# A graph-attention and expert kernel on one Trainium2 core: setup transfers of 125 rows cut in 112 and 13, one queue for x, stores and weights, and the first three pairs summed in plain fp32 with row releases of their own

## The reference, cut to what matters

```python
x = x + gnn(layernorm(x), dist, W, att_src, att_dst, src, dst)      # x: 6250 x 256, 106250 edges
x = x + ffn(layernorm(x)[None], Wr, br, W1, b1, g1, be1, m1, v1, W2, ..., Wo, bo)[0]

def gnn(feat, ...):                       # 4 heads of 64
    ft = (feat @ W).reshape(n, 4, 64)
    e = leaky_relu(e_src[src] + e_dst[dst], 0.2)      # e_src, e_dst: ft times an attention row, summed per head
    ex = exp(e - segment_max(e, dst)[dst])
    a = ex / segment_sum(ex, dst)[dst] * dist
    return segment_sum(ft[src] * a, dst)              # dst is sorted

def ffn(x, ...):                          # 8 experts, all of them for every row
    w = softmax(x @ Wr + br)
    h = relu(bn(x @ W1[e] + b1)); h = relu(bn(h @ W2[e] + b2)); y = h @ Wo[e] + bo
    return sum over e of y[e] * w[e]
```

## Time and profile before

| | before |
|---|---|
| median of 3 runs | 1673.95 us (1670.68 to 1675.28) |
| profiled execution, its own time | 1672.18 us |
| its span, first to last instruction | 1670.6 us |
| TensorE busy | 1488.4 us, 89% of the span |
| VectorE, ScalarE, GpSimd busy | 1213.7, 777.6, 1028.3 us |
| moved by DMA | 187.48 MB, mean 112 GB/s |
| mean granted TensorE clock | 0.954 |

### The profile page before, as it was taken

The page is one execution under the profiler, slowest core; times in us unless marked ns, Lnnn a source line. Parts: engine busy times, 40 slices in busy tenths (PEclk is TensorE's granted clock), DMA queues, the critical chain, the costliest instruction groups (busy, mean ns, idle before and its releaser), DMA issues.

```text
span 1670.6 us, 23915 instructions
## 1 busy us (share of the span) xinstructions
PE 1488.4 (89%) x8358; PEld 1292.6 (77%) x8358; DVE 1213.7 (73%) x2207; ACT 777.6 (47%) x1353; POOL 1028.3 (62%) x926
## 2 busy tenths in 40 slices
PE   2664035999999999999999999999999999999998
PEld 2442034888888888888888888888888888888887
DVE  3333266887888888888888888788778877887751
ACT  1232013455545554555555545555555555455543
POOL 1000777777777777777777777777777777777000
PEclk9887556999999999999999999999999999999999
DMA  3332934444443444344444444444444344433000
GB/s 116 104 103 79 303 111 112 128 115 129 111 128 103 129 112 128 103 129 112 122 112 121 118 115 119 114 123 111 123 115 125 106 125 114 125 105 109 20 0 13
DMA packets 106040, 187.48 MB, mean 112 GB/s; under 512 B 38454, under 2 KB 70475, under 8 KB 105890
## 3 DMA queue, kind: packets, MB, share of 16 engines
q0 software_dynamic: 43664, 121.77, 26.5%
q1 hardware_dynamic: 55264, 57.76, 11.5%
q10 hardware_dynamic: 6992, 6.42, 1.3%
HBM read 172.72 MB, written 14.42 MB: 112 GB/s over the span
## 4 chain that ended last, share of the span: by engine, by line
PE 66%; DVE 11%; issue 7%; DMA 6%; POOL 4%; ACT 4%; SPq 0%; DVEq 0%; ACTq 0%; POOLq 0%
PE bankH L701 33%; PE bankY L730 16%; PE bankE L660 5%; PE bankE L661 5%; POOL gath L565 4%; DMA gath<-in_x 4%; ACT msg_hi L866 3%; DVE onehot L1237 2%; PE bankE L596 2%; PE bankB L646 1%; DVE x L1348 1%; DVE stats L1297 1%; DVE x L1295 1%; DVE x L1291 1%; PE bankA L678 1%
## 5 line engine op out<-in xcount | busy, mean ns | idle before, releaser
L565 POOL DMA_INDIRECT gath<-table,src_win x900 | 1020.9, 1134 | 502.4 <-issue 229.4
L894 ACT ACTIVATE h<-bankH,bn_shift,bn_scale 128x250 f32<-128x250 f32 x800 | 401.5, 552 | 424.6 <-PE bankH L701 424.3
L701 PE MATMUL bankH<-h,w 128*128 128x250 f32 x1600 | 446.6, 398 | 0.0
L730 PE MATMUL bankY<-wo,h 128*125 128x256 f32 x1600 | 378.1, 379 | 1.1 <-DVE x L1348 1.1
L701 PE MATMUL bankH<-xT,w 128*128 128x250 f32 x1600 | 375.2, 377 | 0.1
L1279 DVE TENSOR_TENSOR msg_lo<-gath,msg_hi 128x2340 fp32r<-128x2340 f32 x100 | 259.5, 2595 | 114.3 <-ACT msg_hi L866 114.3
L730 PEld LDWEIGHTS bankY<-wo,h 128*125 128x125 f32 x1600 | 296.0, 187 | 42.5 <-issue 1.4
L866 ACT ACTIVATE msg_hi<-gath 128x2340 fp32r<-128x2340 f32 x100 | 215.1, 2151 | 233.0 <-PE bankE L661 229.6
L701 PEld LDWEIGHTS bankH<-xT,w 128*128 128x128 f32 x1600 | 294.2, 190 | 30.4 <-ACT h L894 0.2
L701 PEld LDWEIGHTS bankH<-h,w 128*128 128x128 f32 x1600 | 278.4, 198 | 18.0 <-issue 0.2
L1348 DVE SCALAR_TENSOR_TENSOR x<-bankY,gate,x 125x256 f32<-125x256 f32 x400 | 173.9, 475 | 136.4 <-PE bankY L730 136.4
(11 more groups left out here) (164 smaller groups left out, 870.1 us busy)
## 6 DMA issues: line engine op xcount, KB each, us to landing
onehot_t<-dst_low SPq DMA_DIRECT2D x50, 576.0 KB, 5.2
gath<-table,src_win POOLq DMA_INDIRECT x900, 2.8
x_res<-in_x SPq DMA_DIRECT2D x27, 250.0 KB
table<-gath SPq DMA_DIRECT2D x25, 253.9 KB
out<-x SPq DMA_DIRECT2D x25, 250.0 KB
gath<-in_x SPq DMA_DIRECT2D x23, 250.0 KB
w<-in_L_ffn_W ACTq DMA_DIRECT2D x2, 2048.0 KB, 21.6
wo<-in_L_ffn_Wo ACTq DMA_DIRECT2D x1, 2048.0 KB, 37.3
```

The source lines that it names most:

```text
L565: pool.indirect_dma_start(gath[:, g.slot(u), t, :], None, table, bass.IndirectOffsetOnAxis(src_win[:, g.win, u, t:t + 1], 0)).then_inc(row ...
L701: mm = pe.matmul(target[:, hc * 2 * NT:(hc + 1) * 2 * NT], weights[:, e * KC + c, hc * P:(hc + 1) * P], operand(c), start=(c == 0), stop=( ...
L730: mm = pe.matmul(bankY[0:NT, u * D:(u + 1) * D], h2[:, e % 2, c, u, :], wo[:, e * KC + c, :], start=(c == 0), stop=(c == KC - 1))
L894: ins = act.activation(target[:, e % 2, hc, :, :].rearrange("p u n -> p (u n)"), source[:, hc * 2 * NT:(hc + 1) * 2 * NT], ACT.Relu, bias= ...
```

## The change

Setup:
- x is loaded in six groups of 1, 1, 2, 4, 8 and 9 pairs, issued at the start with no waits between them, each cut in 112 and 13 rows; stores are cut in the same way. Small parameters and the weights move to SP's queue, the weights in twelve parts of 0.5 MB behind the stores of pairs 4 to 15. W and the attention rows move to ScalarE's queue.
- The norm is two pairs behind the moments, `project` has two sets of banks, and TensorE and ScalarE are one pair further apart. VectorE's steps for edges and factors are spread over pairs 3 to 21 (`aside`).
- GpSimd loads the windows and dst_low of pair 0 itself, before it waits for the stores.

Main part:
- Stage n=-2 is replaced by `first`, which also makes the edge terms of pair 1.
- Pairs 0 to 2 are summed in plain fp32 straight from the gathered rows: one matmul a column and no `keep_high` and `low_part`.
- `Plan` moves steps: for pairs 1 and 2 the run maxima, carries and logits come in the stage in which the pair is g, at s=2 and 3 (pair 1) and 1 and 2 (pair 2), after `layer1` of the pair before has begun. From pair 3 on all is as before.
- The 36 rows of pairs 1, 2 and 3 are released by lists of events.

```diff
+NATIVE = 3
+ROWS_CUT = ((0, 112), (112, NT))
+X_GROUPS = (0, 1, 2, 4, 8, 16, 25)
+SOON = ((2, (0,)), (3, (1,)), (4, (2,)), (5, (3,)))
+STEADY = Plan(0, dict(SOON), 1, 3, {3: (0,), 4: (1,), 5: (2,), 6: (3,)}, {5: (0,), 6: (1,)}, 7)
+PLANS = {0: Plan(0, dict(SOON), 1, 3, {3: (0,), 4: (1,), 5: (2,), 6: (3,)}, {5: (0,), 6: (1,)}, 6, low=False),
+         1: Plan(3, {5: (0,), 6: (1, 2, 3)}, 4, 5, {6: (0,), 7: (1, 2, 3)}, {7: (0, 1)}, 8, runs=2, low=False),
+         2: Plan(2, {4: (0, 1), 5: (2, 3)}, 3, 4, {5: (0, 1), 6: (2, 3)}, {5: (0,), 6: (1,)}, 7, runs=1, low=False)}
...
+        def load_x(eng, k):
+            lo, hi = X_GROUPS[k:k + 2]
+            for p0, p1 in ROWS_CUT:
...
+                eng.dma_start(target, x.rearrange("(k p) d -> p k d", p=NT)[p0:p1, lo * 2:hi * 2, :]).then_inc(t_x[k], 16)
...
             def store_rows(g):
                 sp.wait_ge(t_kept, g.n * 2 + 2)
-                sp.dma_start(table_pairs[g.n], ft_rows[0:NT, g.par, :, :]).then_inc(t_stored[g.par], 16)
+                for p0, p1 in ROWS_CUT:
+                    sp.dma_start(table_pairs[g.n, p0:p1], ft_rows[p0:p1, g.par, :, :]).then_inc(t_stored[g.par], 16)
+            def store_and_load(g):
+                store_rows(g)
+                i, q = divmod(g.n - WEIGHTS_AT, 4)
+                if 0 <= i < 3:
+                    buf, dram = ((w1, W1), (w2, W2), (wo, Wo))[i]
+                    sp.dma_start(buf[:, q * 4:q * 4 + 4, :], ...).then_inc(weights_in, 16)
...
             general(pool, path)
-            pool.wait_ge(setup_done, 1)
+            load_window(pool, Pair(0))
+            pool.wait_ge(low_stored, 32)
+            for u in range(2):
+                load_low(pool, Pair(0), u)
+            pool.wait_ge(t_stored[0], 32 * ((NP + 1) // 2))
+            pool.wait_ge(t_stored[1], 32 * (NP // 2))
+            second = released((
+                (carry_ready, 1, 2), (logit_ready, 1, 2), (ex_ready, 1, 3), (msg_ready, 1, 2), (msg_ready, 2, 2), (msg_ready, 3, 2),
+                (onehot_ready, 5, 2), (msg_ready, 4, 2), (var_ready, 1, 3), (onehot_ready, 7, 2), (var_ready, 2, 2), (xn_ready, 2, 1),
+                (xT_ready, 1, 3), (rexp_ready, 1, 2), (h1_kept, 2, 2), (h2_kept, 1, 2), (h1_kept, 3, 2)))
...
             def project(g):
                 pe.wait_ge(t_xT, g.n + 1)
-                if not g.begins(1):
-                    pe.wait_ge(t_rows, g.n * 2)
+                if not g.begins(2):
+                    pe.wait_ge(t_rows, (g.n - 1) * 2)
...
-                        mm = pe.matmul(bankE[u][0:NT, 0:ROWX], xT[:, g.par, c, u, :], wx[:, c, :],
+                        mm = pe.matmul(t_bank[g.par][u][0:NT, 0:ROWX], xT[:, g.par, c, u, :], wx[:, c, :],
...
             def aggregate(g, c):
+                if g.begins(NATIVE):
+                    pe.wait_ge(msg_ready, g.n * CHUNKS + c + 1)
+                    u, cols = c // 2, (c % 2) * TC
+                    for t in range(TC):
+                        mm = pe.matmul(bankE[u][0:NT, 0:ROW], onehot[:, c, t, :].bitcast(F32), gath[:, g.slot(u), cols + t, :],
+                                       start=(cols + t == 0), stop=(cols + t == TE - 1))
+                    mm.then_inc(agg_done, 1)
+                    return
...
+                    if late(g) and s == plan.logits:
+                        turn_carry(g)
...
+                    if late(g) and s == plan.runs:
+                        turn_runs(g)
```

More of the change, by code:

```diff
@@ L412, in load_dst_low @@
             def load_dst_low(a, u):
[L414 to L418, removed]
+                sp.wait_ge(edge_done, a.tile(u) - 1)
+                load_low(sp, a, u)
             def store(f):
@@ L515, in pace @@
+            assert len(second) == len(third) == len(fourth) == 2 * TE
             def pace(g, row):
-                if g.begins(1):
+                if g.n in early:
+                    event = early[g.n].get(row)
+                    if event is not None:
+                        pool.wait_ge(*event)
                     return
[L519 to L545, removed]
@@ L546, in pace @@
-                if r or not rows:
+                f, step, kind, r = Pair(g.n - 3), FROM, 0, row
+                while r >= BEHIND[step % EX][kind]:
+                    r -= BEHIND[step % EX][kind]
+                    step, kind = (step, kind + 1) if kind < 3 else (step + 1, 0)
+                f, step = f + step // EX, step % EX
+                if r:
                     return
@@ L737, in nothing, with first @@
                 pass
+            def first(a):
+                turn_bounds(None, a)
+                for _ in to_edges(a):
+                    pass
+                ahead = to_edges(a + 1)
+                for _ in range(TE):
+                    next(ahead)
+                turn_runs(a)
+                turn_carry(a)
+                for _ in ahead:
+                    pass
             def body(f, g, a):
-                small = to_edges(a) if a is not None else iter(())
+                small = to_edges(a) if f is not None and a is not None else iter(())
+                plan = plan_of(g)
                 def between():
@@ L790, in _ @@
             general(pe, path)
-            over_stages(NP, body)
+            over_stages(NP, first, body)
             last = Pair(NP - 1)
@@ L940, in path @@
+                    if late(g) and s == plan.logits:
+                        exp_logits(g)
+                    if g is not None and plan.low:
+                        for c in plan.sums.get(s + 1, ()):
+                            keep_high(g, c)
             def path():
@@ L1390, in body @@
                         edge_sum(a)
                         carries(a)
-                    if f is not None and (s >= 2 or not f.begins(1)):
+                    if run and (s >= 2 or not f.begins(1)):
                         add_y(*before(f, s, 2))
-            over_stages(NP, body)
+                    if late(g) and s == plan.runs:
+                        runs(g)
+                    if late(g) and s == plan.logits:
+                        weigh(g)
+            over_stages(NP, first, body)
```

603 lines of the change are left out of this document (354 added, 249 removed).

## The result

| | before | after |
|---|---|---|
| median | 1672.50 us (4 runs, 1670.68 to 1675.28) | 1622.04 us (4 runs, 1620.49 to 1624.87) |
| ratio to before, 95% interval | | 0.9705 [0.9692, 0.9718] |
| profiled execution, span | 1670.6 us | 1620.1 us |
| first gather of pair 0 | 165.6 us | 115.0 us |
| from there to layer 1 of pair 0 | 110.1 us | 81.5 us |

The kernel became 50.5 us faster. That is inside the range and 24 us above the number. So setup holds most of the miss.

The account below looks back on a forecast made before the run. TensorE bounds the main part, and x on one queue with a third of the DMA engines bounds setup; -70.6 - 26 + 13.5 + 7 = -76.1 us, giving 1596.1 profiled and 1598 us predicted, range 1577 to 1632.

Parts of the forecast that it names:

- The cut: Setup loads and stores: 125 rows use 5 of 16 DMA engines, 112 rows use 16 and 13 rows 13.
- First gather at 95: End of setup: pair 0's first gather at 95 us against 165.58, -70.6 us; bounds 84 and 118.
- the 7.5 put down for stalls in it: Setup loop: 3 us for an emptied buffer, 1.5 for small matmuls, 3 for stores with weight parts.
- Pair 0 to layer 1 at 84: First gather to layer 1 of pair 0: 84 us against 110.1, -26 us; bounds -30 and -12.
- The end of the bounds at which all sums run at half clock: Pair 0's sums: 36 matmuls at 0.9 us, 32 us for 18.5, leaving a gain of only 12 us.
- Plain fp32 +13.5: Sums of pairs 1 and 2 in TensorE-bound stages: 16 us a pair against 9.4, +13.5 us for both.
- New waits +7: First main stages: 3.5 us at `turn_runs(1)` and 3.5 for pair 1's chunks, norm and messages; bounds 0 and 25.
- The slower: Setup: the cut doesn't raise the queue's 103 GB/s, first gather at 190, 1693 us; chance 0.02.
- no-gain cases: Setup: the cut brings nothing and the order hides it, first gather near 165, 1670 us; chance 0.01.
- TensorE's half clock: Setup: half clock throughout bounds it, first gather 49 us later, 1647 us; chance 0.07.
- The second rival: Setup: the queue bounds it at 157 GB/s, first gather at 127, 1630 us; chance 0.10.
- The releases: Pairs 1 and 2: event-held rows starve gathers, costing 45 us instead of 7, 1636 us; chance 0.09.

Follow-up runs that it names:

- e1: The kernel before with only its setup x loads and table stores cut in 112 and 13 rows; 1626.8 us.
- e2: The kernel after without the cut, loads and stores of 125 rows again; 1669.8 us.
- e4: e3 with the 16 small parameter loads issued from ScalarE's queue behind the attention rows; 1613.4 us.
- e3: The kernel after with the last x group (9 pairs) loaded in three parts behind the first stores; 1614.2 us.
- e7: e4 without the event lists that hold back the gathers of pairs 1 to 3; 1608.8 us.
- e8: e7 with VectorE's one-hots and scans of pair 3 ahead of pair 2's residual and norm; 1602.9 us.
- e6: e5 with maxima, carries and logits of pairs 1 and 2 back in their old stage, plain fp32 kept; 1620.0 us.
- e5: The kernel after without the event lists that hold back the gathers of pairs 1 to 3; 1615.0 us.

## Why the prediction was right, and where it was off

**The cut (right).** That transfers of 125 rows kept a third of the engines busy, and that this bounded setup, is what e1 and e2 show, from both sides. That it was 5 engines is read from the share (0.33 and 0.34) and the rule cited above; no trace names them.

**First gather at 95 (off by 20, setup's gain mis-sized).** The term that failed is the start of the loop, "All of x needs 21 us and is far ahead of its use". TensorE turns pair 5 from 53.43 us; at the forecast pace, with the first product done at 19, it would have begun at 19 + 4 x 2.65 = 29.6. Of these 24 us 8 were lost before pair 2, which is turned from 30.1 in place of 21.7. There x was not ahead of its use: VectorE waits for the group of pairs 4 to 7, with the DMA engines full, but at 173 to 208 GB/s and not at 304.

```profile
28.20 0.75 DVE L1090 BATCH_NORM_STATS2 stats<-gath 125x6 f32<-125x256 f32 x2 [6.57 <-DMA gath<-in_x]
...
20.00:25.00 5.00, 4.59 (x12) 3.22 (x12) 0.24 (x2) 1.00 (x4) 0.00 (x0) 1.00 1.09 208
25.00:30.00 5.00, 0.00 (x0) 0.00 (x0) 1.73 (x8) 0.99 (x5) 0.00 (x0) 1.00 1.00 173
```

The other 15 are the wait for the first store. The last group is ahead of its use, and that is the fault, for what is ahead of its use here stands in front of the first store on the one queue. Bytes were summed over the whole queue (64 us), but not up to the first store. The step "16 small transfers ... lie under the loop at 0.5 us an issue" left out that SP issues them before its first store, between 26.85 and 36.1 us; in e4, without them in front, the store goes out at 27.6 in place of 38.6. From the restart on the loop runs as worked out, 2.8 us a pair against 2.65 (pair 24 is turned at about 106.8), and 4 us of the 7.5 put down for stalls in it were not needed, so the miss is 20 and not 24. e3 took 4 us of it back in its profile (8 in the median). With the first gather at 103.9 to 107.3 in e4, e7 and e8 about 10 remain, and most of them are the start again: in all three pair 2 is turned from 29.7 to 30.1. No run varied that.

**Pair 0 to layer 1 at 84 (right).** 81.5. The sums of pair 0 are in the chain after:

```profile
169.10 2.56 DVE gath L1384
171.80 6.51 PE bankE L738 x18
178.53 11.85 PE bankE L738 x54
...
196.45 3.72 PE bankH L786 x8
```

One cold chunk of 6.51 us and three in 11.85, 18.4 in all against 18.5. The end of the bounds at which all sums run at half clock, to which the Trainium skill ("TensorE: Matmul & The Clock Gate", HAM oscillation) pointed, did not come here.

**Plain fp32 +13.5 (right).** e6: 6.7 us a pair, 13.4 for two.

**New waits +7 (off by 8).** The two stages of the kernel after grew by 28.5 us over those of before. The lines between which they are counted:

```profile
207.25 0.49 PE L780 MATMUL bankE<-bo_rows,gate_t 32*125 32x256 f32 x2
280.53 0.38 PE L780 MATMUL bankE<-bo_rows,gate_t 32*125 32x256 f32 x1
350.27 0.38 PE L780 MATMUL bankE<-bo_rows,gate_t 32*125 32x256 f32 x1
```

That is 73.28 and 69.74 us. 13.4 of the 28.5 are plain fp32, so 15.1 are waits beyond those of before; stages of 66 and 60 us had been forecast. The wait at `turn_runs(1)` was forecast at 3.5 and is 4.11. Two things were missing. The prediction weighed the half clock for setup and for pair 0, and not behind the wait that it had itself forecast at 3.5 us; two stalls, of 4.11 and 3.85 us, were followed by 4.91 and 6.03 us of work at 0.50, which cost 5.5 us together. Here the warning of the Trainium skill (the section named above) that a throttle comes back after a wait was right, at another place than the one that the prediction gave it. And the wait at `turn_runs(3)`, 6.9 us with its half clock, was not seen, because it comes from VectorE's order and not from the gathers: pair 3 was taken to be as before.

**The rivals.** The slower and the no-gain cases are refuted by e1. TensorE's half clock did not hold through setup; 0.66 between 40 and 60 us is the effect of the store's delay, for in e4, without it, the clock there is 1.00. The second rival had its mechanism half right: ScalarE did wait for a store of two pairs before. But it did so once for 16.3 us and not at a rate of 157 GB/s all through: 152 and 155 GB/s moved from 20 to 60 us, but 277 from 60 to 100. The releases starved no gathers by half, but cost 5 to 7 us (e5, e7).

## What to carry to other kernels

Count the outermost size of each transfer first: one cut of 125 rows into 112 and 13 gave nine tenths of a change that rewrote the whole start. When loads and stores share one queue, sum the bytes and issues up to the first store on which an engine waits, and not only over the queue; a load that is early for its user is late for whoever stands behind it. And price a new wait on TensorE by what follows it too: two of about 4 us cost some 7 each.

## What the runs showed of the hardware beyond what was expected

Issuing is not free behind a large transfer. SP's own times in the kernel after, from the chain of work:

```profile
4.47 1.29 SPq L386
5.80 8.72 SPq L386
...
14.56 1.44 SPq L386
...
26.85 1.15 SPq L416
28.05 1.44 SPq L417
...
33.74 0.49 SPq L422
```

These are the groups of 4 and 8 pairs of x, each as 112 and then 13 rows, and the first small loads; the part of 13 rows of the 8 pairs is the 10.76 us shown at the top. What takes long is not the large part (1.29 and 1.44 us for 0.9 and 1.8 MB) but the small one behind it: 8.72 and 10.76 us for 0.1 and 0.2 MB. In e2 the load of 8 KB behind the group of 8 pairs took 18.04 us to issue. So an engine's own list can stop at a transfer that it only wants to hand over, and the size of that transfer does not tell it.

The Trainium skill ("DMA: Bandwidth & Descriptors", Queues, rings and completion order) says that each engine takes a queue's work in the order in which it was put there; the store that stood behind 2.25 MB and took 11.96 us, where the last one took 2.40, agrees with it.
